# Two-layer convolution block: the first layer's instructions of TensorE, ScalarE and VectorE in another order

## The reference

```python
def _L0_conv_ref(x, w_in, w_dw, fft_weight, w_out):      # HID = 170, P = 8
    h = jnp.einsum('oi,bihw->bohw', w_in, x)
    gate, x_sp, x_fr = jnp.split(h, 3, axis=1)
    sp = jax.lax.conv_general_dilated(x_sp, w_dw, ...)   # depthwise, 3 x 3
    xp = x_fr.reshape(b, HID, H // P, P, W // P, P).transpose(0, 1, 2, 4, 3, 5)
    f = jnp.fft.rfft2(xp) * fft_weight
    fr = jnp.fft.irfft2(f, s=(P, P)) ...                 # back to pixels
    fused = jax.nn.gelu(gate, approximate=False) * (sp + fr)
    return jnp.einsum('oi,bihw->bohw', w_out, fused)

x = x + _L0_conv_ref(_gn(x), ...)
x = x + _L1_conv_ref(_gn(x), ...)    # a state-space layer along rows and along columns
```

## Time and profile before

| | us |
|---|---|
| median of 3 runs (10250.67 to 10262.34) | 10253.36 |
| the profiled execution | 10252.34 |
| its span | 10250.5 |
| TensorE busy | 9482.5 (93%) |
| VectorE busy | 8275.4 (81%) |
| ScalarE busy | 6046.8 (59%) |
| GpSimd busy | 1782.1 (17%) |

### The profile page before, as it was taken

The page is one execution under the profiler, slowest core; times in us unless marked ns, Lnnn a source line. Parts: engine busy times, 40 slices in busy tenths (PEclk is TensorE's granted clock), DMA queues, the critical chain, the costliest instruction groups (busy, mean ns, idle before and its releaser), DMA issues.

```text
span 10250.5 us, 187671 instructions
## 1 busy us (share of the span) xinstructions
PE 9482.5 (93%) x73254; PEld 6605.6 (64%) x73254; DVE 8275.4 (81%) x12487; ACT 6046.8 (59%) x9559; POOL 1782.1 (17%) x1824
## 2 busy tenths in 40 slices
PE   1899988999899998998989999899898999989998
PEld 1677765656577775565667777565566777656555
DVE  7788878878688887887868888787886888878786
ACT  0666654555666665454766666545476666545556
POOL 0000003333300001333320000233341000032333
PEclk9999989999999999998999999899999999989999
DMA  4667666575676766557567776646666666574655
GB/s 112 148 142 146 141 137 207 172 228 157 157 150 142 146 142 172 180 169 233 156 152 146 142 146 142 201 161 194 187 178 130 129 130 129 120 224 161 216 166 156
DMA packets 1333116, 1651.84 MB, mean 161 GB/s; under 512 B 845180, under 2 KB 1077260, under 8 KB 1246860
## 3 DMA queue, kind: packets, MB, share of 16 engines
q1 hardware_dynamic: 1332236, 1639.84, 63.7%
HBM read 786.58 MB, written 514.86 MB: 127 GB/s over the span
## 4 chain that ended last, share of the span: by engine, by line
PE 80%; DVE 10%; ACT 4%; issue 3%; DMA 1%; SPq 1%; POOL 1%; DVEq 0%; ACTq 0%; POOLq 0%
PE ps L823 14%; PE ps L1766 14%; PE ps L1779 7%; PE ps L790 6%; PE ps L1790 5%; PE ps L781 5%; PE ps L837 4%; DVE S L1546 3%; PE ps L856 3%; PE ps L881 3%; PE ps L1414 2%; PE ps L868 2%; PE ps L1335 2%; PE ps L817 2%; PE ps L884 2%
## 5 line engine op out<-in xcount | busy, mean ns | idle before, releaser
L1152 DVE SCALAR_TENSOR_TENSOR F<-U,LW,F 106x512 f32<-106x512 f32 x2048 | 1536.0, 750 | 54.5
L1766 PE MATMUL ps<-fp,Dwr 128*128 128x512 f32 x6144 | 1546.6, 401 | 0.0
L1766 PEld LDWEIGHTS ps<-fp,Dwr 128*128 128x128 f32 x6144 | 1115.6, 188 | 613.5 <-ACT x L1855 292.1
L1130 DVE TENSOR_TENSOR Z<-ps,LW 128x340 f32<-128x340 f32 x1024 | 522.7, 510 | 741.5 <-PE ps L790 721.5
L1855 ACT ACTIVATE x<-ps,cst 128x512 f32<-128x512 f32 x512 | 351.8, 687 | 1012.9 <-PE ps L1779 1009.0
L823 PE MATMUL ps<-P,WP 128*128 128x512 f32 x3072 | 905.7, 417 | 31.8 <-DMA H<-P 31.8
L823 PE MATMUL ps<-H,WP 128*128 128x512 f32 x3072 | 916.7, 420 | 0.0
L1414 PE MATMUL ps<-fp,Bwr 128*128 128x512 f32 x3072 | 877.0, 425 | 21.5 <-DVE fp L1515 21.5
L1779 PE MATMUL ps<-XP,Cwr 128*128 128x512 f32 x3072 | 802.7, 398 | 78.3 <-DVE XP L1901 78.3
L950 ACT ACTIVATE XF<-ps 128x340 f32<-128x340 f32 x1024 | 466.4, 455 | 682.3 <-PE ps L781 681.6
L1070 POOL TENSOR_SCALAR xo<-xo 64x512 f32<-64x512 f32 x4 | 6.0, 1500 | 4835.7 <-DVE xo L1186 4835.7
(11 more groups left out here) (300 smaller groups left out, 19816.7 us busy)
## 6 DMA issues: line engine op xcount, KB each, us to landing
H<-P SPq DMA_DIRECT2D x512, 585.0 KB, 7.2
raw<-x SPq DMA_DIRECT2D x240, 640.0 KB, 11.5
fx_d<-fx SPq DMA_DIRECT2D x112, 1024.0 KB, 3.9
fl_d<-fp SPq DMA_DIRECT2D x112, 1024.0 KB, 5.6
fp<-fl_d SPq DMA_DIRECT2D x112, 1024.0 KB, 6.4
fx<-fx_d SPq DMA_DIRECT2D x112, 1024.0 KB, 5.5
x1h_d<-xo SPq DMA_DIRECT2D x256, 256.0 KB, 9.0
x1v_d<-xo SPq DMA_DIRECT2D x512, 128.0 KB, 8.0
```

Source lines behind the costliest of these rows:

```text
L1130: e.tensor_tensor(Z[t % 2][:, 2 * c:2 * c + 2, :].rearrange("p a b -> p (a b)"), ps[6][:, 0:2 * HID], Wt, ALU.mult).then_inc(sem["z"], 1)
L1152: ins = e.scalar_tensor_tensor(o, u, wd[0:106, i:i + 1], o, ALU.mult, ALU.add)
L1766: ins = e.matmul(bank(m)[:], Dwr[:, w, c:c + 128], fq[n % 2][x][:, s2, :], start=(s2 == 0 and w == 0 and x == 0), stop=False)
```

## The change: what it does

In the steady loop each engine issues the same instructions for a tile as before, in another order. On TensorE, conv is called block by block (its waits are now tied to blocks 0, 2 and 4, and the same calls can hold them singly), one block of bank ps3 more is done ahead for tile t + 1, and wout is cut in two: wout with the two woA matmuls, right behind finv, and wout42 with the other three, later. On VectorE the nine depthwise taps, formerly dealt as 4, 3 and 2, stand singly between other instructions, fu42 is cut into add42 and fu42, bn comes a tile later, x1 behind p2, and fl42 of the last tile stands behind the loop. Tap 0 waits for the fl42 of two tiles before. On ScalarE columns comes ahead of the first xf, rows works for t + 1 in place of t + 2 and stands ahead of the second xf, ge(t, 1) comes behind it. The prologue and the special cases of the last tile change along.

```diff
@@ l0_pe: conv
-            if blocks[0] == 0:
-                if i == 0:
+            col = 64 * i
+            for j in blocks:
+                if j == 0:
                     e.wait_ge(sem["p2"], NT * b + t + 1)
-                if t:
-                    e.wait_ge(sem["fu"], 2 * (NT * b + t - 1) + i + 1)
-            col = 64 * i
-            if blocks[0] == 2 or i and blocks[0] == 0:
-                h_there(e, b, t)
-            for j in blocks:
+                    if t:
+                        e.wait_ge(sem["fu"], 2 * (NT * b + t - 1) + i + 1)
+                if j == 2:
+                    h_there(e, b, t)
                 if j == 4:
-                    if i == 0:
-                        e.wait_ge(sem["xr"], NT * b + t + 1)
+                    e.wait_ge(sem["xr"], NT * b + t + 1)
@@ l0_pe: prologue
         xs(0, 0)
-        conv(0, 0, range(2))
+        conv(0, 0, range(1))
         conv(0, 1, range(2))
+        fs(0, 0)
+        xs(0, 1)
         for k in range(3):
             pointwise(0, k)
         e.matmul(ps[4][0:106, :], w(0, W_U, 106), HH[0][:, 0, 0:512], start=True, stop=True)
-        fs(0, 0)
-        conv(0, 0, range(2, 5))
-        xs(0, 1)
-        conv(0, 1, range(2, 3))
         fs(0, 1)
-        conv(0, 1, range(3, 5))
         xs(0, 2)
-        gate(0, 0)
-        gate(0, 1)
         fs(0, 2)
-        gate42(0)
         xs(0, 3)
         fs(0, 3)
@@ l0_pe: loop
         for t in range(NT):
-            if t:
-                gate(t, 0)
-                gate(t, 1)
-                conv(t, 0, range(2, 5))
+            conv(t, 1, (2,))
+            gate(t, 0)
+            conv(t, 1, (3,))
+            conv(t, 0, (1, 2))
             xs(t + 1, 0)
-            if t:
-                conv(t, 1, range(3))
+            gate(t, 1)
+            conv(t, 0, (3,))
             fs(t + 1, 0)
-            if t:
-                conv(t, 1, range(3, 5))
+            conv(t, 1, (4,))
+            conv(t, 0, (4,))
+            xs(t + 1, 1)
             finv(t)
-            xs(t + 1, 1)
-            if t:
-                gate42(t)
+            wout(t - 1)
             fs(t + 1, 1)
+            gate42(t)
             pointwise(t + 1, 0)
+            xs(t + 1, 2)
             pointwise(t + 1, 1)
-            xs(t + 1, 2)
-            if t == NT - 1:
-                finv42(t)
-            wout(t - 1)
+            pointwise(t + 1, 2)
             fs(t + 1, 2)
-            pointwise(t + 1, 2)
-            conv(t + 1, 0, range(1))
+            conv(t + 1, 0, (0,))
+            conv(t + 1, 1, (0,))
+            wout42(t - 1)
             xs(t + 1, 3)
-            if t < NT - 1:
-                finv42(t)
-            conv(t + 1, 0, range(1, 2))
+            finv42(t)
             fs(t + 1, 3)
+            conv(t + 1, 1, (1,))
         wout(NT - 1)
+        wout42(NT - 1)
@@ l0_act
         xf(0, 0)
+        xf(0, 1)
         for k in range(3):
             uc(0, k)
+        xf(0, 2)
         blocks(1)
-        rows(1)
-        for c in range(1, 4):
-            xf(0, c)
+        xf(0, 3)
         for t in range(NT):
+            if t >= 3 and t % 2:
+                columns((t - 3) // 2)
+            xf(t + 1, 0)
             ge(t, 0)
-            ge(t, 1)
-            xf(t + 1, 0)
             fh42(t - 1)
             ... interleave, as before ...
-            if t >= 3 and t % 2:
-                columns((t - 3) // 2)
+            rows(t + 1)
             xf(t + 1, 1)
+            ge(t, 1)
             ge42(t)
+            xf(t + 1, 2)
             uc(t + 1, 0)
+            p1(e, b, t + 2)
             uc(t + 1, 1)
-            xf(t + 1, 2)
-            p1(e, b, t + 2)
             uc(t + 1, 2)
             xf(t + 1, 3)
             blocks(t + 2)
-            rows(t + 2)
@@ l0_dve: loop
         for t in range(NT):
+            depthwise(t, (4,))
             z(t + 1, 0)
-            depthwise(t, range(4, 7))
+            bn(t - 2)
+            depthwise(t, (5,))
             fu(t, 0)
+            depthwise(t, (6,))
+            z(t + 1, 1)
+            depthwise(t, (7,))
             fu(t, 1)
-            z(t + 1, 1)
+            depthwise(t, (8,))
             fl42(t - 1)
-            depthwise(t, range(7, 9))
             z(t + 1, 2)
-            if t == NT - 1:
-                fu42(t)
-            x1(t - 1)
             if t == 60: ...
             p2(t + 2)
+            depthwise(t + 1, (0,))
+            x1(t - 1)
+            depthwise(t + 1, (1,))
+            add42(t)
+            depthwise(t + 1, (2,))
             z(t + 1, 3)
-            if t < NT - 1:
-                fu42(t)
-            else:
-                fl42(t)
+            depthwise(t + 1, (3,))
+            fu42(t)
             ... gn1_dve, as before ...
-            bn(t - 1)
-            depthwise(t + 1, range(4))
+        fl42(NT - 1)
+        bn(NT - 2)
         x1(NT - 1)
```

More of the change, by code:

```diff
@@ L877, in wout, with wout42 @@
                 e.wait_ge(sem["x1"], NT * b + t)
-            s = t % 2
-            m = F128[s][:].rearrange("c i (a q w) -> c q a i w", q=2, w=64)
+            m = F128[t % 2][:].rearrange("c i (a q w) -> c q a i w", q=2, w=64)
             for p in range(2):
                 e.matmul(ps[7][64 * p:64 * p + 64, :], woA, m[:, p], start=True, stop=False, skip_group_check=True)
+        def wout42(t):
+            if t < 0:
+                return
+            s = t % 2
             e.wait_ge(sem["fl42"], NT * b + t + 1)
@@ L1148, in depthwise @@
                     e.wait_ge(sem["uc"], 3 * (NT * b + t) + 3)
+                    if t >= 2:
+                        e.wait_ge(sem["fl42"], NT * b + t - 1)
                     ins = e.tensor_scalar(o, u, wd[0:106, 0:1], None, ALU.mult)
@@ L1153, in depthwise, with add42 @@
                 ins.then_inc(sem["tap"], 1)
-        def fu42(t):
+        def add42(t):
             e.wait_ge(sem["fi42"], NT * b + t + 1)
@@ L1158, in fu42 @@
             e.tensor_tensor(F42[t % 2][:], ps[4][0:106, :], F42[t % 2][:], ALU.add).then_inc(sem["ad"], 1)
+        def fu42(t):
             e.wait_ge(sem["ad"], NT * b + t + 1)
```

## The result

The changed kernel takes 10153.81 us (median of 4, 10152.52 to 10156.14) against 10255.32 us (median of 4, 10250.67 to 10262.34): a ratio of 0.9901, 95% interval 0.9884 to 0.9918. The forecast was 10187, range 10120 to 10260, faster. The profiled execution took 10152.52 us, its span is 10150.6 us against 10250.5: 99.9 us less, where 65.5 were forecast.

What follows compares the result with a forecast made beforehand. TensorE was taken to set the pace at 18.46 us a tile. Steady tiles -66, starts -12.5, ends -6 and interleave +19 total -65.5 us on 10252.34: 10187 us, range 10120 to 10260.

Steps and rivals of the forecast that it cites:

- link of the chain: Steady tile, xs to XF to fs to Z to next xs: 1.12 us needed behind xs, 1.34 behind fs; none late.
- both waits for XF: TensorE's fs(t+1,0) and fs(t+1,1) wait for ScalarE's XF; the new order removes 0.11 + 0.09 = 0.20 us a tile.
- its slack: VectorE in the steady tile: its 15.9 us of work don't grow, and about 1.8 us stay free.
- B: Rival, chance 0.09: three links stay just in time, 0.10 us each; 18.46 us a tile, 10253 us, no change.
- C: Rival, chance 0.08: VectorE becomes the bound at 19.3 us a tile; 10457 us, about 10325 for half the excess.
- The crossing: TensorE, finv beside woA: one way out and in go, a quarters-to-halves step comes; 0.10 us a tile saved.
- rival A: Chance 0.17: finv-to-woA step free, ScalarE catches up before the interleaved tiles' fs1, z0 in time; -25, -19, -7: 10136 us.
- fs(t+1,0) to xs(t+1,1): Steady-tile link: xs may start 1.34 us behind fs, the order gives 1.50; tight, so +0.03 us, between 0 and 0.10.
- The layout: TensorE's new order laid out by hand from the tile's start, fs3 at 16.71, ending at about 18.2 us.
- the sum: Steady tile -0.20 - 0.10 + 0.03 = -0.27 us, so 18.19; 61 tiles x 4 images make -66 us.
- The interleave: ScalarE, tiles 0, 1, 2 and 4 of images 2 to 4: fs1 1.6 us late, +19 us (bounds 0 and 30).
- The starts and ends: Each image's starts -12.5 us (bounds 0 and -24), its last x1 earlier, -6 us (bounds +4 and -12).

Runs made afterwards that it cites:

- Experiment 5: Kernel before, with wout cut in two and its woA matmuls moved right behind finv, all else in the old order: 10229.64 us, ratio 0.9983.
- experiment 6: Kernel before with wout cut and woA right behind finv, plus xf(t+1,0) ahead of the two gelus on ScalarE: 10209.72 us, ratio 0.9963.
- Experiment 4: Changed kernel with VectorE's nine taps dealt as 3, 2 and 4 in rows instead of singly: 10220.96 us, ratio 0.9969.
- experiment 3: Changed kernel with finv42 moved up behind finv and woA, conv blocks in its place, z(t+1,3) one tap earlier: 10089.54 us, ratio 0.9840.
- experiment 1: Changed kernel with ScalarE's interleave in tiles 0, 1, 2 and 4 of images 2 to 4 moved behind ge(t,1): 10132.38 us, ratio 0.9884.

## Why the prediction was right, and where it was too small

**The mechanism held.** No link of the chain is late in the steady tile; both waits for XF are gone, 0.20 us a tile by the rows' lengths as said (0.18 by the distance from each fs to the next start); VectorE has its slack; rivals B and C did not come. Experiments 5 and 6 show in the old kernel that the parts can be had one by one, and that what one link gains another may lose. That it is the even spacing of the four links that lets the new order keep both 0.20s is my reading; no run changes the spacing alone.

**The crossing was sized wrong.** The step in question is "No row has such a step; its bounds are 0 and 0.20 us, and I take 0.10". The step from finv to woA costs nothing: finv takes 1.09 us up to its neighbour whether that is woA or xs, and woA behind it has no extra in front. So 0.20 us a tile was saved, not 0.10, which is rival A's term: 25 us of the miss. I had weighed the Trainium skill there, TensorEngine Tiling (Array Packing), section Tiling Modes, Key Properties: changing the tiling mode drains TensorE. For the ways into and out of the full array the traces agree, 0.10 us each; for quarters to halves they show no cost, so for this step the measurement decides: if TensorE drains there, it costs nothing that the distances show.

**fs(t+1,0) to xs(t+1,1)** was given 0.03 us for being tight. It comes 1.51 us behind (1021.40 to 1022.91) and costs nothing: 7 us. The sum of these steps is -0.40; measured is -0.389 a tile, or about -96 us over the 62 tiles of each image behind the first, the last one apart, where -66 were forecast for 61.

**The layout was better than the sum.** The prediction's own layout ends with fs3 at 16.71, and 0.55 + 0.10 + 0.705 behind it make 18.07, not "about 18.2". Measured from the same point, the starts of the matmul groups lie within 0.06 us of it (xs1 at 6.45 for 6.40, woA at 8.04 for 8.10, fs3 at 16.69 for 16.71), apart from those directly behind an fs, where the layout books the cost of fs otherwise; the tile is 18.08. It prices the crossing at 0.09 and still comes out right, since it gives 0.04 too little ahead of fs0 and as much again behind woA: that part is luck. But 18.07 against the 18.19 of the sum was a contradiction that could be seen beforehand.

**Not in the sum at all:** tiles 60 and 61. They took 19.4 us each before, since ScalarE waited 4.1 us with p1 for VectorE's copy of the last row's padding; counted from the tile's gate(t,0), the copy comes 3.5 us earlier on VectorE now and ScalarE is ready for p1 1.0 us earlier, so the wait is 1.6 us, and TensorE doesn't wait behind it. With tiles 41 and 51, which in images 1 to 3 carried a second gn1 for 0.2 us, about -9 us.

**The interleave was sized wrong the other way.** +19 were forecast. Tiles 1, 2 and 4 of three images cost +15 (1.5 to 1.7 each, forecast 1.6), but tile 0 costs 4.8, 4.8 and 3.7 over image 1's tile 0 instead of 1.6, since ScalarE's table load stands in the same queue and the clock fell behind the idle time: +28 in all. The prediction leaves the table load out.

**The starts and ends** came out at about -11 (forecast -12.5) and -5 (forecast -6), after the 0.7 us are put back and the steady gain of tiles 1 to 4 is taken off.

Together: -96 - 9 + 28 - 11 - 5 - 7 (the second layer) = -100 against -99.9. The forecast was two thirds of the gain. That tiles 60 and 61, left out, and the interleave, 9 us too small, cancel is luck, and so are the 7 us of the second layer; what is left of the miss is the steady tile.

**The taps.** That they stand singly was argued only from VectorE's slack. Experiment 4 puts a number on one other order, 0.32 us a tile: there the 1.68 us of idle time before z(t+1,0) turn into a wait of TensorE. Since it moves five taps ahead of z(t+1,0) as well, it doesn't show what dealing them singly is worth by itself; groups that stand behind z(t+1,0), as in the kernel before, were not tried.

The Trainium skill, VectorE: DVE Perf Modes, section The DRAIN you can't avoid, reports that eight copies take the same time with a semaphore after each as with one after the last. That is the price of giving a signal, which every tap does in all these orders. What the traces here show is the price of awaiting one: the starts of two taps lie 0.79 us apart when the second awaits the first, and four kinds of instruction that don't await it (z, fu, fu42, fl42) come 0.66 behind a tap. Awaiting isn't the whole of it: add42 comes 0.77 behind its tap (1033.52 to 1034.29), though it awaits nothing of it; its other wait, for finv42, isn't the reason, since the distance is the same in experiment 3, where finv42 ends 8.7 us before. That cause is open.

## What to carry to other kernels

When an engine reads as 100% busy, measure the distances between starts against an undisturbed neighbour of the same kind; here 0.4 us of an 18.5 us tile, and with experiment 3 0.67 us, lay in waits and changes of array shape that the busy time hides. Put work on part of the array side by side, and space the links of a chain through several engines evenly; when one is moved, look at what the neighbours of its old place lose. Work that only the first tiles carry needs a check of its own against the new order.

## What the hardware showed that I had not expected

- Going from the full array to part of it and back costs about 0.10 us each way, but from quarters to column halves nothing, and woA is 0.10 us shorter when work of its own shape follows (0.91 for 1.01 us).
- In tile 0 of image 2 of the changed kernel a stall of 3.08 us on TensorE was followed by a stretch of 4 us at a mean granted clock of 0.65 (between the levels of 2.4 and 1.2 GHz), and the next four groups of matmuls took 4.56 us (2768.57 to 2773.13) where they take 3.0 in a steady tile: the stall cost half its length again. In experiment 6 the stall of 2.47 us in the same tile was followed by 3 us at 0.50; in experiment 1, without the stall, the clock stayed at 1.00.
- Of VectorE's taps, one that awaits the tap before it starts 0.79 us behind it; most instructions that don't await it start 0.66 us behind, one (add42) 0.77.
